# One store per unit for the intermediate of a two-layer normalised convolution

## The reference

```python
x = x + conv3x3(group_norm(x), L0_weight) + L0_bias   # 4 groups of 2 channels
x = x + conv3x3(group_norm(x), L1_weight) + L1_bias
```

## Time and profile before

| what | value |
|---|---|
| median of 3 runs | 3917.45 us (3915.92 to 3917.98) |
| the profiled execution, its own time | 3912.56 us |
| its span in the profile | 3910.9 us |
| PE busy | 3472.6 us, 89% of the span |
| ACT busy | 1711.4 us, 44% |
| DVE busy | 1430.8 us, 37% |
| POOL busy | 592.4 us, 15% |
| DMA: moved, mean rate | 1344.32 MB, 344 GB/s |
| DMA: share of 16 engines, loads, stores, statistics | 40.7%, 35.2%, 18.2% |

### The profile page before, as it was taken

How to read it: one execution, slowest core, us unless ns; L and a number is a source line. 1 busy time by engine, 2 the same in 40 slices (tenths; PEclk the granted TensorE clock), 3 DMA queues, 4 the chain that set the end, 5 groups by cost and what they waited for, 6 DMA issues and landing times. The chain is left out here.

```text
span 3910.9 us, 216983 instructions
## 1 busy us (share of the span) xinstructions
PE 3472.6 (89%) x99136; PEld 1837.6 (47%) x99136; DVE 1430.8 (37%) x2460; ACT 1711.4 (44%) x1553; POOL 592.4 (15%) x1061
## 2 busy tenths in 40 slices
PE   0698999989899898998989989898998989999898
PEld 0354545445454454544445445454544445455454
DVE  7555224542245322553225432254223552223300
ACT  0243444434444343444444434444444435444444
POOL 0111111111111111111111111111111111111111
PEclk9998999999999999999999989999999989999999
DMA  9698999989989898998989989899898989999798
GB/s 344 241 385 300 404 375 337 363 302 414 354 334 359 315 415 298 385 349 334 409 293 391 337 341 415 296 390 344 349 395 296 382 308 388 387 281 309 250 312 269
DMA packets 334124, 1344.32 MB, mean 344 GB/s; under 512 B 38800, under 2 KB 38928, under 8 KB 301200
## 3 DMA queue, kind: packets, MB, share of 16 engines
q10 hardware_dynamic: 149648, 537.60, 40.7%
q0 software_dynamic: 147456, 536.94, 35.2%
q1 hardware_dynamic: 36864, 268.45, 18.2%
HBM read 805.45 MB, written 536.87 MB: 343 GB/s over the span
## 5 line engine op out<-in xcount | busy, mean ns | idle before, releaser
L391 PE MATMUL conv<-x_tile,wts 32*32 32x512 f32 x49152 | 3382.9, 601 | 138.2 <-DVE bias L541 17.1
L396 PE MATMUL conv<-x_tile,wts 32*32 32x512 f32 x49152 | 3405.2, 603 | 2.4 <-issue 2.4
L391 PEld LDWEIGHTS conv<-x_tile,wts 32*32 32x32 f32 x49152 | 1597.8, 103 | 1681.4 <-issue 1368.1
L330 ACT ACTIVATE out_tile<-conv,bias 128x1024 f32<-128x1024 f32 x512 | 570.7, 1115 | 1960.7 <-PE conv L396 1946.7
L455 DVE BATCH_NORM_STATS2 bn_mid<-out_tile 128x6 f32<-128x512 f32 x1024 | 658.8, 685 | 963.8 <-ACT out_tile L330 711.9
L396 PEld LDWEIGHTS conv<-x_tile,wts 32*32 32x32 f32 x49152 | 958.5, 103 | 78.5 <-issue 3.5
L447 DVE BATCH_NORM_STATS2 bn_x<-stat_tile 128x6 f32<-128x512 f32 x896 | 550.2, 679 | 963.0 <-DMA stat_tile<-x_dram 963.0
L334 ACT ACTIVATE out_tile<-conv,bias 64x1024 f32<-64x1024 f32 x512 | 569.1, 1111 | 13.3
L332 ACT ACTIVATE out_tile<-conv,bias 64x1024 f32<-64x1024 f32 x512 | 567.1, 1108 | 13.2
L232 POOL DMA_DIRECT2D mid_dram<-out_tile x512 | 272.9, 533 | 1538.9 <-ACT out_tile L330 1051.6
L232 POOL DMA_DIRECT2D out_dram<-out_tile x512 | 268.1, 524 | 1558.4 <-ACT out_tile L330 1086.7
(11 more groups left out here) (45 smaller groups left out, 115.1 us busy)
## 6 DMA issues: line engine op xcount, KB each, us to landing
stat_tile<-x_dram SPq DMA_DIRECT2D x256, 1024.0 KB, 9.7
mid_dram<-out_tile POOLq DMA_DIRECT2D x512, 512.0 KB, 8.5
out_dram<-out_tile POOLq DMA_DIRECT2D x512, 512.0 KB, 9.1
x_tile<-x_dram ACTq DMA_DIRECT2D x504, 512.0 KB, 12.1
x_tile<-mid_dram ACTq DMA_DIRECT2D x504, 512.0 KB, 11.8
x_tile<-x_dram ACTq DMA_DIRECT2D x8, 480.0 KB, 6.7
x_tile<-mid_dram ACTq DMA_DIRECT2D x8, 480.0 KB, 6.1
x_tile<-pad_row ACTq DMA_DIRECT2D x16, 32.0 KB
```

What stands on the lines that cost most here:

```text
L330: act.activation(out_tile[:, slot, 0], conv[:, parity, 0], ACT.Identity, bias=bias[:, 0:1]).then_inc(evicted, 1)
L391: nc.tensor.matmul(columns_of(parity, i, q, c), wts[part, MAIN, kw], rows_of(TILE * q, TILE, slot, c, kw), start=first, stop=end)
L396: last = nc.tensor.matmul(columns_of(parity, i, q, 1 - c), wts[part, ABOVE, kw], rows_of(TILE * above, TILE, slot if q else (slot - 1) % S ...
```

## The change

In layer 0 a unit's two blocks leave in one transfer of 1 MB, which waits for all three evictions of the unit. Layer 1 keeps its two transfers of 512 KB. `stores_before`, the number that the `stored` semaphores must have reached, counts 16 for a unit of layer 0 in place of 32. In SBUF the two blocks of a slot lie side by side in each partition; in `mid` they are 512 KB apart, and the access pattern goes partition by partition, the two blocks of one partition one after the other.

```diff
--- before.py
+++ after.py
@@ -152,7 +152,8 @@
 
         def stores_before(n, g):
 
-            return 32 * (2 * UNITS // RING * n + g // RING)
+            turns = UNITS // RING
+            return 16 * 3 * turns * n + 16 * (min(g // RING, turns) + 2 * max(g // RING - turns, 0))
 
         def evicts_through(n, g, parts):
             return EVICTS * 2 * UNITS * n + (EVICTS * g + parts + FREE)
@@ -220,16 +221,20 @@
             alone(pool.tensor_scalar(mid_group[:, :], same_group[:, 0:CH:GROUP_CH],
                                      float(ROWS * GROUP_CH * GROUPS), 0.0, ALU.mult, ALU.add))
 
-            def store(n, g, i):
-                layer, u = divmod(g, UNITS)
-                row = ROWS * (2 * u + i)
-                if layer == 0:
-                    to = mid[bass.ds(n, 1), CH * row:CH * (row + ROWS), :].rearrange("n a w -> (n a) w")
-                else:
-                    to = out_by_row[row:row + ROWS, bass.ds(n, 1)].rearrange("r n c w -> r (n c) w")
+            def store_mid(n, g):
+                row = 2 * ROWS * g
+                pool.wait_ge(evicted, evicts_through(n, g, EVICTS))
+                pool.sem_inc(results_seen)
+                pool.dma_start(mid[bass.ds(n, 1), CH * row:CH * (row + 2 * ROWS), :]
+                               .rearrange("n (b p) w -> (n p) b w", b=2),
+                               out_tile[:, g % RING]).then_inc(stored[g % RING], 16)
+
+            def store_out(n, g, i):
+                row = ROWS * (2 * (g - UNITS) + i)
                 pool.wait_ge(evicted, evicts_through(n, g, EVICTS if i else 1))
                 pool.sem_inc(results_seen)
-                pool.dma_start(to, out_tile[:, g % RING, i]).then_inc(stored[g % RING], 16)
+                pool.dma_start(out_by_row[row:row + ROWS, bass.ds(n, 1)].rearrange("r n c w -> r (n c) w"),
+                               out_tile[:, g % RING, i]).then_inc(stored[g % RING], 16)
 
             with pool.Fori(0, IMAGES) as n:
                 for g in range(2 * UNITS):
@@ -238,8 +243,11 @@
                         pool.sem_inc(results_seen)
                         pool.tensor_scalar(pad_row[0:CH, :], zeros[0:CH, :], own_mean[0:CH, 0:1],
                                            None, ALU.add).then_inc(pad_row_filled, 1)
-                    for i in range(2):
-                        store(n, g, i)
+                    if g < UNITS:
+                        store_mid(n, g)
+                    else:
+                        for i in range(2):
+                            store_out(n, g, i)
 
         @block.scalar
         def _(act):
```

## The result

The changed kernel takes **3928.47 us** (median of 7 runs, 3921.37 to 3938.39) beside 3917.45 us before: a ratio of **1.0028**, 95% interval 1.0016 to 1.0039. A second set, beside 21 runs of the kernel before, gave 1.0038 (1.0025 to 1.0052). So the change costs 11 to 15 us. The profiled execution was the slowest of its seven, 3938.39 us with a span of 3936.8, so a difference of two totals from the traces exaggerates; I compare stretches.

What follows compares the result with a forecast made beforehand. PE's pace (busy 89%) and the chains between layers were taken to bound the kernel. All terms came to 0: 3912.6 + 0 = 3912.6 us, with the median of runs 4.9 us above, so 3918; range 3899 to 3937.

Steps and rivals of the forecast that it cites:

- rival B: Layer 0 beside statistics: loads run longer without stores, 1.26 us per pair of units, 3935 to 3970 us; chance 0.15.
- Removed: Layer 0: 256 of 512 store issues on POOL and 4096 completion records go; worth 0 us.
- Moved: Layer 0: the first block's store is issued 2.27 us later, behind L334; costs 0 us.
- Added: Layer 0: a single 1 MB transfer, 1.1 us to issue on POOL, rows alternating 512 KB apart; no change.
- 36 us as the most to be won: Late data in layer 0 of seven images with statistics loads: 36 us, the most that changing layer 0's traffic can win.
- Rival A: Layer 0: loads get 2.27 us more before stores compete; half of 36 us comes back, 3900 us; chance 0.15.
- Rival C: Layer 0: merged transfer counts double in queue rotation, loads' share falls; 1.7 us per pair, 3989 us; chance 0.10.
- Its own sign: Layer 0: store queue with about twice the packets of the load queue when both are full.

Runs made afterwards that it cites:

- Late only: Kernel before, with both 512 KB stores of a layer 0 unit issued behind its last eviction, not merged: 3918.06 us, 0.9994.
- changed, again: The changed kernel run once more without edit, in a second set beside the kernel before: 3933.5 us, 1.0038.
- two by partition: Changed kernel with its 1 MB transfer cut into two of 512 KB, each over 64 partitions and both blocks: 3940.13 us, 1.0059.
- three stores: Kernel before, with layer 0's block 1 stored in two halves of 64 partitions, each behind its own eviction: 3903.81 us, 0.9958.
- three, block 1 late: Kernel before, with layer 0's block 1 stored in two halves of 64 partitions, both behind the last eviction: 3901.95 us, 0.9964.
- four stores: Kernel before, with four 256 KB stores per layer 0 unit: block 0's behind L330, block 1's each behind its own half: 3906.87 us, 0.9971.
- four late: Kernel before, with four 256 KB stores per layer 0 unit, all behind the unit's last eviction: 3929.34 us, 1.0033.

## Why the prediction came out as it did

The time, 3928.5 us, lies inside the range of 3899 to 3937. The likeliest case, no change (3918, at 0.54), was not what came: the kernel is slower by 0.28%, past the 0.2% named as the bound, to which the prediction gave 0.28. That the range holds the time is luck in part: its upper end comes from rival B, whose cause is not the one that acted.

**Removed, POOL's issues and the completion records: right.** 92 us less work on POOL and 4096 fewer packets on the queue bought nothing.

**Moved, 2.27 us later: right, and shown.** "Late only" is the move alone and took 0.9994. The waits at units 4, 28 and 32 and for the ring of four slots stayed covered: no eviction waits for a store in the changed kernel, and the transfers behind the other three are issued at most 0.3, 0.5 and 1.0 us after the unit's first eviction, as before.

**Added, the single transfer at no cost: this is the step that failed.** The prediction set the alternating rows at "no change" because a window of stores ran at 416 GB/s. That row says how fast the stores go, and they do go as fast. The DMA view of the changed kernel, 3517 to 3518.5 us, image 7, mostly stores, moves 410 GB/s:

```profile
q0 software_dynamic: 131, 0.49, 80.8%
q10 hardware_dynamic: 31, 0.13, 21.5%
```

The cost appears with the loads beside them. The term measures 15 to 18 us, all in layer 0 beside statistics loads, and 0.1 us in image 7. It arises between units 8 and 24, as the excess of the seven layers 0 by stretch shows, in us over 6.74 for a unit, the pace of image 7 (in brackets the number of waits):

```
kernel                whole   units     last     PE's waits for x
                              8 to 24   unit     before units 9 to 24
before                 36.5    29.2     -0.2     14.4 (25)
late only              35.8    28.5     -0.2     11.9 (22)
changed                51.6    44.0     -0.1     25.4 (39)
changed, again         54.4    46.3     -0.1     22.3 (34)
two by partition       50.9    32.5      9.6     14.5 (22)
three stores           18.3    10.7     -0.1      3.7 (7)
three, block 1 late    17.1     9.8      0.3      2.3 (5)
four stores            16.1     6.9      6.4      0 (0)
four late              38.2    16.5     15.5      0.5 (1)
```

**36 us as the most to be won: right so far as tried.** The best kernel still has 16 to 18 us of it.

**Rival A** didn't happen: loads wait more, not less. **Rival C** didn't either: packets on the store queue are 4 KB, and the layers grew by 2 us and not by the 10 of that case. Its own sign is absent too. I counted packets of data in units 8 to 24 of images 1 to 6, half a microsecond or more inside the stretches in which loads and stores both ran and no statistics load did: 1.08 of the store queue for one of the load queue before, 1.08 and 1.07 in the two executions of the changed kernel, and 1.03 in "late only". The Trainium skill (DMA: Bandwidth & Descriptors, section Queues, rings and completion order) has an engine drain one ring's packet of 9 to 17 descriptors before the next ring's, and the prediction weighed that a merged store's 16 rows on an engine would then go in one turn. These counts give that reading no support, and no run here shows how many rows an engine takes in one turn.

**Rival B**, the gap, had the symptom and not the cause. I sorted the time of units 8 to 24 of layer 0, in images 1 to 6, into steps of 0.05 us, by which of the three queues kept two or more of the 16 engines busy. In us per layer:

```
kernel               loads, no stores   loads + stores    16 units
                     (with/without      (with/without
                      statistics)        statistics)
before                   21.1               80.9            112.5
late only                21.5               78.2            112.2
changed                  26.5               74.7            114.8
changed, again           25.5               76.1            114.7
two by partition         21.6               79.8            112.9
three stores             16.2               85.3            109.8
three, block 1 late      15.9               84.8            109.6
four late                10.9               86.3            110.4
```

In each of these kernels loads alone move 267 to 292 GB/s, loads with statistics 318 to 349, loads with stores 388 to 404, and all three 364 to 373. So the rates of rival B are right. The changed kernel has 5 us more per layer in the slow mixes, and the 16 units take 2.3 us longer, 14 us in six images. Rival B worked this out from a start 2.27 us later, but "late only" starts as late and has no longer gap. Its sign was a layer of 216 to 221 us in images 1 to 6; the changed kernel has 213.8 to 217.8.

What is shown: the cost is the merging and not the lateness. It arises between units 8 and 24 of the layers 0 with statistics loads, and there it goes when the statistics loads are spread. Cutting the merged transfer in two by partition takes back 12 to 14 of the 16 to 18 us that it costs in this stretch over "late only", in the excess, in PE's waits for `x` and in the loads alone (21.6 us beside 21.5 and 26.5). The alternation between the two blocks, which that kernel keeps, doesn't bring the cost by itself, and the single transfer of 1 MB is the nearest suspect. That much is indicated and not shown.

What in the transfer would act is open. It isn't a larger share of the engines, by the counts above. Its start isn't enough: in image 7 its first packet comes 1.28 us after the issue in place of 1.11 in "late only", but in the stretch that loses time the store queue was still at work at 93 of 96 issues (images 1 to 6). And the alternation isn't cleared, since the halves of 64 partitions may win back what it costs: block 1 in such halves gains 18 us beside the kernel before, and four late stores, which have the halves and not the alternation, have only 16.5 us of excess in this stretch. A single transfer that writes one block after the other would separate them, and wasn't tried. Open as well is why cutting block 1 in two gains these 18 us when block 0 leaves early, and why ACT issues its loads more slowly and the last unit is longer when all halves leave late.

## What to carry to other kernels

A wait table that shows nobody waiting for a transfer says that its own duration is free, not that its shape is: with the DMA queues full, the shape of the stores moved the whole kernel by 0.4% down and 0.3% up, though nobody waited for a store in the three versions concerned. Before merging transfers to save issues, ask whether the issuing engine was on the path at all. Where three queues share the engines, try the opposite as well: here three smaller stores per unit gained 0.42%, one large store lost 0.28%, and four small late ones lost 0.33%. And read a difference by stretch before you put it down to a theory: the whole of "two by partition" speaks for one cause, its stretches for another.

## What the runs showed of the hardware

- Loads of `x`, whose channels lie 4 MB apart, run at 254 GB/s alone; with stores beside them the two together run at 408. In 3.5 us of the changed kernel (672.6 to 676.1 us) the loads moved 0.68 MB, 194 GB/s, and the stores 0.76 MB beside them. What the distance of 4 MB has to do with the 254 was not tested.
- A store of 1 MB from POOL is issued in 0.71 us where two of 512 KB take 0.53 each: the time of an issue did not double with the rows.
- Four transfers of 256 KB per unit made ACT wait for their slots (108.9 us in 31 waits, 149.6 us in 39 when late), though the bytes are the same.
- The shape of POOL's stores changes how long ACT needs to issue a load of `x`: over 1 us in 93 of 512 issues with two late stores of 64 partitions and in 79 with four, against 5 before.
- In the first unit of a layer, with little else in the queues, the order of service is closer to that of arrival than to equal turns. I read this from the packets by half microseconds in image 1: the 1 MB of statistics was served alone, then the first load alone, and only then did the second load and the first store alternate.
